# Decoder layer on one core: gate and up columns loaded into the array from DRAM tile by tile, products left unturned, down product one step nearer

## The reference

```python
logits = xt @ Ws + bs                       # 1600 x 8
topk_w, topk_idx = jax.lax.top_k(logits, 2)
topk_w = jax.nn.softmax(topk_w, axis=-1)
combine = sum(one_hot(topk_idx, 8) * topk_w[..., None], axis=1)
g = einsum('td,edf->tef', xt, Wg)           # Wg, Wu: 8 x 256 x 688
u = einsum('td,edf->tef', xt, Wu)
h = silu(g) * u
y = einsum('tef,efd->ted', h, Wd)           # Wd: 8 x 688 x 256
out = einsum('ted,te->td', y, combine)
x = layernorm(x + out)
```

## Time and profile before

| | us |
|---|---|
| median of 3 runs | 719.72 (718.25 to 720.38) |
| time of the profiled execution | 723.84 |
| its span, first to last instruction | 721.9 |
| attention block, about | 0 to 422 |
| routing and first gather | 422 to 434 |
| 32 tiles of the experts, TensorE's part | 434.25 to 699.80 |
| last additions, last norm, output | 699.80 to 721.9 |

### The profile page before, as it was taken

The page is one execution under the profiler, slowest core; times in us unless marked ns, Lnnn a source line. Parts: engine busy times, 40 slices in busy tenths (PEclk is TensorE's granted clock), DMA queues, the critical chain, the costliest instruction groups (busy, mean ns, idle before and its releaser), DMA issues. The chain is left out here.

```text
span 721.9 us, 15610 instructions
## 1 busy us (share of the span) xinstructions
PE 645.6 (89%) x5190; PEld 494.8 (69%) x5191; DVE 381.0 (53%) x975; ACT 315.6 (44%) x761; POOL 287.8 (40%) x522
## 2 busy tenths in 40 slices
PE   6988977999999989999899729999999999999960
PEld 5887855677777767777677516777777777777750
DVE  2878765777777866787677641222222222222214
ACT  2344333677777766777676512222222222222202
POOL 3435454433333376336742321334333333334323
PEclk9999986999999998999999958999999999999995
DMA  8232114455556556555555550111221122112205
GB/s 255 76 77 73 55 34 125 130 167 163 169 170 173 160 152 188 167 163 163 145 147 144 186 214 23 26 31 28 33 36 30 30 31 35 29 30 30 28 1 182
DMA packets 60831, 73.95 MB, mean 102 GB/s; under 512 B 9498, under 2 KB 50786, under 8 KB 60002
## 3 DMA queue, kind: packets, MB, share of 16 engines
q1 hardware_dynamic: 54626, 65.53, 30.7%
q0 software_dynamic: 6144, 7.61, 6.5%
HBM read 38.38 MB, written 12.44 MB: 70 GB/s over the span
## 5 line engine op out<-in xcount | busy, mean ns | idle before, releaser
L1443 DVE TENSOR_REDUCE cmx<-ps 100x1 f32<-100x361 f32 x256 | 134.5, 531 | 69.5 <-PE ps L956 65.2
L1233 ACT ACTIVATE cpr<-ps 128x300 f32<-128x300 f32 x256 | 104.7, 419 | 57.6 <-PE ps L967 57.0
L1739 POOL DMA_INDIRECT accd<-y,si x32 | 51.3, 1602 | 137.4 <-DVE y L1962 137.4
L1950 DVE TENSOR_TENSOR hh<-sg,ps 128x344 f32<-128x344 f32 x64 | 32.8, 513 | 113.5 <-PE ps L1811 113.5
L956 PE MATMUL ps<-st 96*100 96x361 bf16 x256 | 85.7, 338 | 6.5 <-DMA st<-parts 3.1
L1833 PE MATMUL ps<-WD,hT 128*128 x384 | 88.3, 380 | 1.4 <-DVE y L1962 0.7
L1811 PE MATMUL ps<-WG,xsT 128*128 x256 | 86.3, 460 | 0.6 <-ACT xsT L1867 0.6
L1811 PE MATMUL ps<-WU,xsT 128*128 x256 | 85.6, 457 | 0.0
L967 PEld LDWEIGHTS ps<-st 120*128 120x128 bf16 x768 | 62.8, 102 | 31.6 <-issue 8.8
L1833 PEld LDWEIGHTS ps<-WD,hT 128*128 128x128 f32 x384 | 72.8, 190 | 16.1 <-issue 1.9
L967 PE MATMUL ps<-st 120*128 120x100 bf16 x768 | 76.8, 208 | 3.3 <-ACT st L1238 1.6
(11 more groups left out here) (219 smaller groups left out, 1104.7 us busy)
## 6 DMA issues: line engine op xcount, KB each, us to landing
st<-parts SPq DMA_DIRECT2D x192, 115.2 KB, 2.5
WD<-in_wd SPq DMA_DIRECT2D x6, 1024.0 KB, 11.5
cx<-in_ctxT SPq DMA_DIRECT2D x16, 361.0 KB, 5.1
WG<-in_wg SPq DMA_DIRECT2D x8, 688.0 KB, 4.7
WU<-in_wu SPq DMA_DIRECT2D x8, 688.0 KB, 4.5
x_sb<-in_x SPq DMA_DIRECT2D x8, 200.0 KB
x1d<-x SPq DMA_DIRECT2D x8, 200.0 KB
x1Td<-x1T SPq DMA_DIRECT2D x8, 200.0 KB, 3.3
```

The costliest lines, as they stand in the source:

```text
L1233: act.activation(pr[:, h % (2 * HG), :], ps[:, B_T + h % 2, 0:NCH * L], ACT.Exp).then_inc(exp_ok, 1)
L1443: dve.tensor_reduce(mx[:, half, hh:hh + 1], ps[0:L, B_S + h % 2, 0:CTX], AX_X, ALU.max).then_inc(max_ok, 1)
L1739: pool.indirect_dma_start(accd, bass.IndirectOffsetOnAxis(ap=si[:, t.par:t.par + 1], axis=0), y[:, t.par, :], None, compute_op=ALU.add, bo ...
L1950: dve.tensor_tensor(hh[:, t.par, f * FH:(f + 1) * FH], sg[:, f, :], ps[:, B_U + f, 0:FH], ALU.mult).then_inc(h_ok, 1)
```

## The change

The diff does these things together:

1. Gate and up weights are laid out on the host as 11 chunks of 128 columns for each expert (4 gate, then gate 4, a shared chunk with the 48 left-over gate and up columns, up 4, then 4 up) and are no longer kept in SBUF for all experts. SyncE fetches one expert's 1408 columns (128 partitions x 2816 values, 1.44 MB) for each tile into one of four slots W, three tiles ahead (`weights`). The first tile always belongs to expert 0 (the `jv` memset), whose weights W0 come during the attention block.
2. In `gate_up` the weight chunk is the loaded operand and xsT is streamed (128 columns). The result has F on partitions already, so `turn_hidden` and its two copies are gone, and VectorE writes the product straight into hT.
3. `down` of tile n stands in step n, between the first part and the rest of gate/up of n+1; so do `weigh` and `add_rows`.
4. WD is loaded in the passes 0 to 5 of the attention block, W0 in pass 6, nothing behind that.
5. The last norm is cut into five pieces, with the root on ScalarE and the reciprocal on VectorE instead of a power on GpSimd.

```diff
@@ attention block, SyncE
-                    for n in range(2 * E):
-                        if i == (n if n < E else n - 1):
-                            W, w = ((WG, wg), (WU, wu))[n % 2]
-                            sp.dma_start(W[:, :, n // 2, :], w[n // 2, :, :].rearrange("(k p) f -> p k f", p=P))\
-                                .then_inc(experts_in, 16)
+                    if 0 <= i < FC:
+                        sp.dma_start(WD[:, i, :, :], wd[:, i, :, :]).then_inc(R.wd_in, 16)
+                    if i == FC:
+                        sp.dma_start(W0[:, :, :], wgu[0, :, :, :]).then_inc(R.wd_in, 16)
...
-                    if i == NB - 1:
-                        for u in range(2):
-                            sp.wait_ge(kq_in[u], 16 * SLOTS * NB)
-                        sp.wait_ge(t_mm, H * (NB - 1))
-                        load_down(range(FC // 2))
...
-                    if i == NB - 1:
-                        load_down(range(FC // 2, FC))
@@ experts block, SyncE
+                def weights(t):
+                    wait(sp, gu_mm, 3 * (t.n - 3))
+                    e = sp.value_load(expert_of[0:1, bass.ds(t.n, 1)], min_val=0, max_val=E - 1)
+                    sp.dma_start(W[t.slot][:, :, :], wgu[bass.ds(e, 1), :, :, :].rearrange("e p k f -> p (e k) f"))\
+                        .then_inc(w_in[t.slot], 16)
+
+                def emit(t, n):
+                    if n == -1:
+                        weights(t + 2)
+                    if n + 3 < TILES:
+                        weights(t + 3)
@@ experts block, GpSimd
-                    if n - 1 >= 0:
-                        add_rows(t - 1)
+                    if 0 <= n < TILES:
+                        add_rows(t)
                     if n + 3 < TILES:
                         gather(t + 3)
@@ experts block, TensorE
-                def gate_up(t, e, halves):
+                def gate_up(t, parts):
                     pe.wait_ge(xT_ev, t.n + 1)
-                    for f in halves:
-                        wait(pe, h_ok, 2 * t.n + f - 1)
-                        for bank, W in ((B_G, WG), (B_U, WU)):
+                    wait(pe, w_in[t.slot], 16 * (t.lap + (t.slot > 0)))
+                    for part in parts:
+                        if part == 0:
+                            wait(pe, sg_ok, 2 * t.n - 3)
+                        else:
+                            wait(pe, h_ok, 2 * t.n - 4 + part)
+                        for i, (kind, _) in enumerate(ORDER[part]):
+                            c = i + sum(len(p) for p in ORDER[:part])
                             for k in range(KC):
-                                mm = pe.matmul(ps[:, bank + f, 0:FH], xsT[:, t.par, k, :],
-                                               W[:, k, bass.ds(e, 1), f * FH:(f + 1) * FH],
-                                               start=(k == 0), stop=(k == KC - 1))
-                            mm.then_inc(gu_mm, 1)
...
+                                mm = pe.matmul(ps[:, bank(t, part), i * P:(i + 1) * P], W[t.slot][:, k, c * P:(c + 1) * P],
+                                               xsT[:, t.par, k, :], start=(k == 0), stop=(k == KC - 1))
+                        mm.then_inc(gu_mm, 1)
...
-                        if c == 0:
-                            pe.wait_ge(hTa_ev, t.n + 1)
-                        if c == 4:
-                            pe.wait_ge(hTb_ev, t.n + 1)
+                        if c == 0:
+                            pe.wait_ge(h_ok, 2 * t.n + 2)
@@ experts block, ScalarE and VectorE
+                    if part == 0:
+                        a = act.activation(sg[:, 0:4 * P], ps[:, bank(t, part), :], ACT.Silu)
+                    else:
+                        act.activation(sg[:, 4 * P:5 * P], ps[:, bank(t, part), 0:P], ACT.Silu)
+                        a = act.activation(sg[U_AT:U_AT + FLEFT, 5 * P:6 * P], ps[0:FLEFT, bank(t, part), P:2 * P], ACT.Silu)
...
+                        dve.tensor_tensor(hT[:, t.par, FULL - 1, :], sg[:, 4 * P:5 * P], ps[:, bank(t, part), 2 * P:3 * P], ALU.mult)
+                        h = dve.tensor_tensor(hT[left, t.par, FULL, :], sg[left, 5 * P:6 * P],
+                                              ps[left, bank(t, part), P:2 * P], ALU.mult)
+                    else:
+                        h = dve.tensor_tensor(hT[:, t.par, 0:FULL - 1, :].rearrange("p c t -> p (c t)"), sg[:, 0:4 * P],
+                                              ps[:, bank(t, part), :], ALU.mult)
@@ last norm, VectorE
+                for q in range(NQ):
+                    sums_of(q)
+                    if q >= 1:
+                        scales(q - 1)
+                    moments(q)
+                    if q >= 1:
+                        shifts(q - 1)
+                normal(9)
+                normal(10).then_inc(scaled_ok, 1)
+                scales(NQ - 1)
```

More of the change, by code:

```diff
@@ L51 @@
 TILES = (2 * T) // P + E - 1
-FH = F // 2
 FC = (F + P - 1) // P
 FP = FC * P
+FULL = F // P
+FLEFT = F - FULL * P
+U_AT = 64
+ORDER = ((("g", 0), ("g", 1), ("g", 2), ("g", 3)), (("g", 4), ("both", 5), ("u", 4)), (("u", 0), ("u", 1), ("u", 2), ("u", 3)))
+GU = P * sum(len(part) for part in ORDER)
 TP = T // P
 TR = T - P * TP
-NQ = 4
-QT = TP // NQ
+PIECES = ((0, 2), (2, 5), (5, 8), (8, 11), (11, TP + 1))
+NQ = len(PIECES)
 VJ = (T + P - 1) // P
@@ L1639, in experts @@
         xsT = sb("xsT", [P, 2, KC, P])
-        sg = sb("sg", [P, 2, FH])
-        hh = sb("hh", [P, 2, FP])
+        sg = sb("sg", [P, 6 * P])
+        W = [W0, *(sb(f"W{u}", [P, KC, GU]) for u in range(1, 4))]
         hT = sb("hT", [P, 2, FC, P])
@@ L1891, in emit, with deviation, apply @@
                     if n + 1 < TILES:
[L1892 removed]
+                        silus(t + 1, 1)
                 steps(emit, act)
[L1895 to L1901 removed]
+                act.activation(warm[:, :], warm[:, :], ACT.Sqrt)
+                def deviation(q):
+                    act.wait_ge(mv_ok, 2 * q + 2)
+                    some = slice(*PIECES[q])
+                    act.activation(dev[:, some], mv[:, some, 1], ACT.Sqrt, bias=eps[:, 0:1]).then_inc(dev_ok, 1)
+                def apply(q, slots):
+                    act.wait_ge(scaled_ok, q + 1)
+                    for j in slots:
+                        r = act.activation(acc[:, j, :], acc[:, j, :], ACT.Identity, bias=shift[:, j:j + 1],
+                                           scale=rstd[:, j:j + 1])
+                    return r
+                deviation(0)
+                deviation(1)
+                apply(0, (0, 1)).then_inc(res_ok, 1)
+                deviation(2)
+                apply(1, (2, 3, 4)).then_inc(res_ok, 1)
+                deviation(3)
+                apply(2, (5, 6))
+                deviation(4)
+                apply(2, (7,)).then_inc(res_ok, 1)
+                apply(3, (8,)).then_inc(res_ok, 1)
             @block.vector
@@ L1982, in last_stats, with sums_of, moments @@
+                steps(emit, dve)
+                def sums_of(q):
+                    dve.wait_ge(acc_ins[q], 32 if q == NQ - 1 else 16)
+                    for j in range(*PIECES[q]):
+                        m = dve.bn_stats(stats[0:rows(j), j, :], acc[0:rows(j), j, :])
                     m.then_inc(mv_ok, 1)
-                    dve.wait_ge(mv_ok, 3 * q + 1)
-                    for j in slots(q):
-                        n = P if j else TR
-                        m = dve.bn_aggr(mv[0:n, j, :], stats[0:n, j, :])
+                def moments(q):
+                    dve.wait_ge(mv_ok, 2 * q + 1)
+                    for j in range(*PIECES[q]):
+                        m = dve.bn_aggr(mv[0:rows(j), j, :], stats[0:rows(j), j, :])
@@ new lines, in shifts, with normal @@
+                def shifts(q):
+                    some = slice(*PIECES[q])
+                    dve.wait_ge(rstd_ok, q + 1)
+                    dve.scalar_tensor_tensor(out=shift[:, some], in0=mv[:, some, 0], scalar=-1.0, in1=rstd[:, some],
+                                             op0=ALU.mult, op1=ALU.mult).then_inc(scaled_ok, 1)
+                def normal(j):
+                    n = rows(j)
+                    return dve.tensor_scalar(acc[0:n, j, :], acc[0:n, j, :], mv[0:n, j, 0:1], rstd[0:n, j:j + 1],
+                                             ALU.subtract, ALU.mult)
@@ L2031, in columns, with gate_up_columns, down_rows @@
         return v.reshape(-1, P).T
+    def gate_up_columns(g, u):
+        w = np.zeros((E, D, GU), g.dtype)
+        for c, (kind, f) in enumerate(chunk for part in ORDER for chunk in part):
+            if kind == "both":
+                w[:, :, c * P:c * P + FLEFT] = g[:, :, FULL * P:]
+                w[:, :, c * P + U_AT:c * P + U_AT + FLEFT] = u[:, :, FULL * P:]
+            else:
+                w[:, :, c * P:(c + 1) * P] = (g if kind == "g" else u)[:, :, f * P:(f + 1) * P]
+        return w
+    def down_rows(d):
+        w = np.zeros((E, FP, D), d.dtype)
+        w[:, 0:FULL * P, :] = d[:, 0:FULL * P, :]
```

(2 more changed lines are left out.)

198 lines of the change are left out of this document (76 added, 122 removed).

## The result

The changed kernel takes 795.07 us (median of 4 runs, 786.58 to 798.87) against 720.05 (4 runs) for the kernel before beside it: ratio 1.1006, 95% interval 1.0916 to 1.1097. The forecast was 715 us, range 705 to 734. It was wrong in its sign.

What follows compares the result with a forecast made beforehand. TensorE (89% busy) was taken as the bound, the gather's chain nearly as long. Span 721.9 - 10.1 (loop) - 2.9 - 0.8 + 14.5 D, D = 0.6, gave 716.8; the median 2.2 lower, about 715 us, range 705 to 734.

Steps and rivals of the forecast that it cites:

- TensorE's step, 7.73: Tile loop: gate/up 4.93, down 2.59 and rows 0.21 make 7.73 us (7.55 to 7.95), 0.36 less than before.
- The gather's chain: Tile loop: down, weigh, addition, gather, rows turned; 7.93 us alone, its excess over TensorE's step shared by two steps.
- the term D: Tile loop: delay the weight fetch costs the gather, taken as 0.6 us (0 to 1.3); a step gets half of it.
- at fair turns: DMA engines alternate between the fetch's rows and the gather, which meets a row's 0.46 us up to three times: 1.3 us.
- It limits itself: Tile loop: a stalled step issues the fetch later, so from a stall of about 1.35 us the gather is first; step at most 9.1.
- rival 2's far end: Tile loop: gather waits until the whole fetch is over, median 742 us; chance 0.12 of the 0.32 for slower.
- The clock: Tile loop: 2.6 us charged for the low clock at the first tile.
- (a): Attention block: the wait before line 1488, behind 3 MB of WD, goes: -2.9 us.
- (b): Start of the loop: three weight fetches beside the first gather, landed in 3.13 us before, lengthen it by the term D.
- (c): End of the kernel: last norm in smaller pieces, shorter first load and last store, -0.8 us (-1.5 to +0.5).
- The wait for VectorE's last product: Before down: about 1.1 us, hidden by 0.7 us under 1.79 us of the next tile's first gate/up part.
- rivals 3 and 4: Tile loop: array load above 0.117 us beside streaming (chance 0.02); or gather's chain always the bound, 709 to 718 us.

Runs made afterwards that it cites:

- the four-fold cuts: Changed kernel with each weight fetch as four DMAs: cut by columns 749.11 us, by blocks of 32 partitions 825.51 us, by every fourth partition 760.64 us.
- the interleaved cut: Changed kernel with each weight fetch as four DMAs of every fourth partition, pieces of 11 KB as in one fetch: 760.64 us, ratio 1.0512.

## Why the prediction was wrong

- **TensorE's step, 7.73: right.** 44 records at 0.112 us, and the tiles without stalls took 251.2 us against 251.0 worked out. (The estimate of 4.71 us beside it in the prediction is 44 loads of 107 ns; were streaming the bound, as the sentence says, it would be 4.75.)
- **The gather's chain: right in form, wrong in size.** The gather became late, and the stall was shared by two steps (the excess, 5.03 + 7.2 - 7.73 = 4.5, falls on every second one). What failed is the term D. I bounded it by 1.3 us "at fair turns" (three times 0.46 is 1.38) and took 0.6. It was 4.4 (7.2 instead of 2.8) in the step shown, and 2.6 to 4.9 whenever a fetch was ahead (landings of 5.4 to 7.7). I had the overlap of the two in time, worked out to the half microsecond, and asked how the engines would share; I should have asked who comes first. The fetch was ahead by 0.68 us.
- **The Trainium skill against the bound.** "DMA: Bandwidth & Descriptors", section "Queues, rings and completion order", says that an engine changes queues only after a whole packet, and I worked out from it that the gather waits until the fetch is over. The 0.14 MB at 579.4 to 581.7 us agree with that. That the four-fold cuts let the gather in halfway agrees too, but order of issue alone would give the same there. I gave it 0.12 because no row before had two queues busy. That was no evidence for fair turns either.
- **"It limits itself": the second step that failed.** I held that the step can't exceed 9.1 us, because a stall delays the fetch too. A stalled step does let the gather through first, but then the next step doesn't stall, its fetch is issued early, and the next gather is shut out. The system alternates between 0 and 2.8 to 4.9 us instead of settling at 1.35. The mean idle time is 1.8 us a step (54.6 over 31), which with the low clock made 10.8 of the two steps shown, where the limit was to be 9.1; so even rival 2's far end, 742 us, fell 53 short. In the kernel before with the fetch added the stalls came in nearly every step, 1.5 us each, so there they did settle. Why one kernel alternates and the other doesn't, no run shows.
- **The clock: not in the sum at all.** I charged the low level only to the first tile. Behind the stalls of 3.3 us and more gate/up ran 1.1 to 2.6 us longer; with the turnings that is some 23 us. Without it the span would be about 761.
- **(a) The wait of line 1488: right in sign.** It went; the first gather was issued at 423.91 instead of 429.76. But executions scatter: eight traces with the new attention block have 420.4 to 427.4 (mean 424.2), three with the old one 427.4 to 429.8 (mean 428.9), so 4.7 rather than 2.9, and not to be had from one pair.
- **(b) First gather, +D: right in form again.** 8.10 us instead of 3.13, which ate (a).
- **(c) The end, -0.8: too small, and outside its own range (-1.5 to +0.5).** It was -2.3; the read-back of the first piece took 3.10 us instead of 4.82.
- **The other bets.** The wait for VectorE's last product stayed hidden; weights were on time; rivals 3 and 4 did not happen.

## What to carry over

Where a long DMA and a short one that someone waits for meet on the same engines, work out which is issued first, and charge the short one with all of the long one; then issue the short one a step earlier, which cost nothing here. Cut a long transfer across its columns, not into blocks of partitions, if it must be cut. Charge a stall with the clock that it costs behind it, and look whether a delay that feeds back settles or alternates.

## What the runs showed of the hardware

- A gather waits for the whole of a fetch issued just ahead of it: uncut, a gather issued 0.68 us behind a fetch of 1.44 MB landed after 7.2 us instead of 2.8; issued 1.3 us ahead of it, after 2.9 (median); with four DMAs for one fetch, after a median of 4.5 and 4.6 us, whatever the length of the pieces. At the start of the loop a gather passed the last of three fetches issued ahead of it.
- A DMA into 32 neighbouring partitions cost 71 us of engine time a MB, into every fourth partition 47. The Trainium skill ("DMA: Bandwidth & Descriptors", section "The descriptor swizzle") gives each write port eight partitions, four neighbours and the four that stand 32 further on, so that 32 neighbours lie at half of the ports. The ratio here is 1.5 over all, and about 830 to 422 ns for the median packet; that the ports are the reason was not tested.
- The granted clock fell after most stalls. The windows of the changed kernel from 561.20 (behind 4.46 us of idling) and from 570.20 (behind none), columns as above:

```profile
561.20:567.60 6.40, 6.40 (x47) 6.40 (x46) 1.27 (x3) 0.93 (x3) 1.17 (x2) 0.79 0.17 35
570.20:575.30 5.10, 5.10 (x47) 5.10 (x46) 1.75 (x4) 0.93 (x3) 2.08 (x3) 1.00 0.43 131
```

0.79 is a mean over both levels (1.2 and 2.4 GHz). Shorter stalls did not always cost it, as TensorE's timeline of the interleaved cut shows, where 2.10 us of idling left gate/up at full speed and 3.24 did not:

```profile
555.54 0.44 PE L1807 MATMUL ps<-ident,xs 128*128 128x128 f32 x2 [2.10 <-DMA xs<-x2d,gi]
555.82 5.08 PE L1824 MATMUL ps<-xsT,W 128*128 128x128 f32 x44
...
574.45 0.69 PE L1807 MATMUL ps<-ident,xs 128*128 128x128 f32 x2 [3.24 <-DMA xs<-x2d,gi]
574.93 6.32 PE L1824 MATMUL ps<-xsT,W 128*128 128x128 f32 x44
```
